# A graph layer's gathers of edge rows: the fourth tile of each group with 127 rows in place of 128

## The reference

```python
h = relu(layernorm(x))
l0, l1 = h0 @ W_l1_0 * a / 8, (h1 @ W_l1_1) * a / sqrt(32)     # the table, 6250 x 160
w = relu(edge_attr_10 @ W_fc1 / sqrt(10)) * sqrt(2) @ W_fc2 / 10   # 192 weights of each edge
y0, y1 = l0[src], l1[src]                                       # the gather, 206250 rows
m0 = w0 * y0 * e0;            m1 = (w1 * y0)[:, :, None] * e1[:, None, :]
m2 = (w2 * e0)[:, :, None] * y1;  m3 = w3 * einsum('eud,ed->eu', y1, e1) / sqrt(3)
s = segment_sum(m, dst)                                         # for each of m0 to m3
out = x + self_interaction(h) + 0.5 * (linear maps of s) * a
```

## Time and profile before

| | before |
|---|---|
| median of three runs | 2132.71 us |
| the profiled execution, its own time | 2139.31 us |
| span of the profiled execution | 2137.5 us |
| PE busy | 2021.8 us (95%) |
| DVE busy | 1684.6 us (79%) |
| POOL busy | 1576.3 us (74%) |
| ACT busy | 343.0 us (16%) |
| mean granted clock of TensorE | 0.928 |

### The profile page before, as it was taken

How to read it: one execution, slowest core, us unless ns; L and a number is a source line. 1 busy time by engine, 2 the same in 40 slices (tenths; PEclk the granted TensorE clock), 3 DMA queues, 4 the chain that set the end, 5 groups by cost and what they waited for, 6 DMA issues and landing times.

```text
span 2137.5 us, 42022 instructions
## 1 busy us (share of the span) xinstructions
PE 2021.8 (95%) x11466; PEld 1603.7 (75%) x11466; DVE 1684.6 (79%) x4634; ACT 343.0 (16%) x636; POOL 1576.3 (74%) x1637
## 2 busy tenths in 40 slices
PE   6899999999999999999999999999999999999998
PEld 5677777787778778777777777777777777777776
DVE  6478878788787888888877888887888878888786
ACT  4311111111111111111111111111111111111111
POOL 6277777777777777777777777777777777777774
PEclk8699999899998998999998989999999989998998
DMA  4223222223222332232232223233232322322233
GB/s 134 72 70 72 72 72 70 71 71 72 71 72 69 71 72 71 70 73 71 71 103 71 71 71 71 72 71 72 71 71 71 73 70 70 73 72 69 71 72 91
DMA packets 159932, 158.29 MB, mean 74 GB/s; under 512 B 86882, under 2 KB 131846, under 8 KB 159914
## 3 DMA queue, kind: packets, MB, share of 16 engines
q0 software_dynamic: 77376, 132.16, 25.0%
q1 hardware_dynamic: 81400, 24.49, 5.2%
q10 hardware_dynamic: 1138, 1.43, 0.2%
HBM read 149.90 MB, written 8.03 MB: 74 GB/s over the span
## 4 chain that ended last, share of the span: by engine, by line
POOL 31%; issue 25%; DMA 18%; DVE 15%; PE 9%; DVEq 1%; POOLq 1%; ACT 0%; SPq 0%; ACTq 0%
POOL y L361 31%; DMA y<-table,idx 17%; DVE hot L654 5%; DVE msg L630 5%; DVE dot L624 4%; PE ps_s L858 2%; PE ps_w L830 2%; PE ps_s L860 2%; PE ps_h L823 1%; DVE dots L620 1%; PE ps_w L792 1%; DVE stats L520 1%; PE ps_h L781 0%; POOLq L369 0%; DVEq L685 0%
## 5 line engine op out<-in xcount | busy, mean ns | idle before, releaser
L361 POOL DMA_INDIRECT y<-table,idx x1612 | 1541.9, 957 | 536.5 <-issue 490.5
L830 PEld LDWEIGHTS ps_w<-w_fc,hr 100*128 100x128 f32 x3224 | 539.3, 197 | 331.8 <-issue 331.8
L830 PE MATMUL ps_w<-w_fc,hr 100*128 100x192 f32 x3224 | 663.0, 351 | 0.0
L858 PE MATMUL ps_s<-hot,msg 128*128 128x128 f32 x3224 | 485.0, 298 | 67.9 <-DVE msg L640 67.3
L858 PEld LDWEIGHTS ps_s<-hot,msg 128*128 128x128 f32 x3224 | 436.6, 206 | 112.3 <-DVE msg L640 109.0
L459 ACT ACTIVATE hr<-ps_h 100x512 f32<-100x512 f32 x403 | 240.7, 597 | 1681.1 <-PE ps_h L823 1681.1
L823 PE MATMUL ps_h<-rad,w_fc 10*100 10x512 f32 x806 | 464.1, 656 | 5.7 <-DMA rad<-in_radial 5.7
L620 DVE TENSOR_TENSOR dots<-y,attr_sb 128x384 f32<-128x384 f32 x403 | 225.1, 559 | 276.7 <-DMA y<-table,idx 276.3
L860 PE MATMUL ps_s<-hot,msg 128*128 128x64 f32 x3224 | 432.0, 280 | 0.0
L860 PEld LDWEIGHTS ps_s<-hot,msg 128*128 128x128 f32 x3224 | 423.3, 205 | 0.0
L682 DVE TENSOR_TENSOR acc<-acc,ps_s 64x32 f32 (+1 forms) x1612 | 325.2, 202 | 71.6 <-PE ps_s L860 31.1
(11 more groups left out here) (79 smaller groups left out, 527.0 us busy)
## 6 DMA issues: line engine op xcount, KB each, us to landing
y<-table,idx POOLq DMA_INDIRECT x1612
rad<-in_radial SPq DMA_DIRECT2D x202, 40.0 KB
xres<-in_x SPq DMA_DIRECT2D x7, 560.0 KB, 4.2
table<-y SPq DMA_DIRECT2D x6, 560.0 KB, 3.2
out<-xres SPq DMA_DIRECT2D x6, 560.0 KB, 4.7
idx<-in_src SPq DMA_DIRECT2D x202, 4.0 KB
attr_sb<-in_attr SPq DMA_DIRECT2D x202, 16.0 KB
dst_i<-in_dst ACTq DMA_DIRECT2D x1, 808.0 KB, 6.3
```

What stands on the lines that cost most here:

```text
L361: nc.gpsimd.indirect_dma_start(out=y[:, j, t, :], out_offset=None, in_=table, in_offset=bass.IndirectOffsetOnAxis(ap=idx[:, j // HALF, col ...
L830: ins = nc.tensor.matmul(ps_w[:, s, t, 0:NW], hr[:, s, t * P:(t + 1) * P], w_fc2[:, :], start=True, stop=True)
L858: nc.tensor.matmul(ps_s[:, s, 0:4 * W], msg[:, s, t, 0:P], hot[:, s, t, 1:V, :], start=(t == 0), stop=(t == T - 1))
```

## The change

The first three tiles of a group keep 128 edges, the fourth has 127 (`ROWS_OF`), so a group holds 511 edges (`EG`). 206250 edges make 404 groups in place of 403, so LEFT is 4 and not 3; TURNS stays 101, and so does the number of SP's loads. The fourth gather of each group goes over partitions 0 to 126 of `idx` and `y`. So that partition 127 of that tile of `y` holds numbers, POOL sets partitions 96 to 127 of it to zero once, after the table's stores have landed and before the first gather. On the host the edges are laid out anew, with attributes of zero in the row that is not used. The compute instructions keep their shapes: they still go over 128 partitions.

```diff
--- before.py
+++ after.py
@@ -29,10 +29,12 @@
 V = 5
 G = 4
 HALF = 2
-TURNS = -(-E // (P * T * G))
+ROWS_OF = [P] * (T - 1) + [P - 1]
+EG = sum(ROWS_OF)
+TURNS = -(-E // (EG * G))
 GROUPS = TURNS * G
 TILES = GROUPS * T
-EDGE_GROUPS = -(-E // (P * T))
+EDGE_GROUPS = -(-E // EG)
 LEFT = EDGE_GROUPS - (TURNS - 1) * G
 PAIRS = TURNS // 2
 assert TURNS == 2 * PAIRS + 1
@@ -150,6 +152,7 @@
         ld_w = sem("ld_w")
         ld_wnode = sem("ld_wnode")
         zeroed = sem("zeroed")
+        y_zeroed = sem("y_zeroed")
         consts = sem("consts")
         dst_step = sem("dst_step")
         base_bc = sem("base_bc")
@@ -349,6 +352,9 @@
             pool.wait_ge(order_step, 3)
             nc.gpsimd.memset(acc[:, :, :], 0.0).then_inc(zeroed, 1)
             pool.wait_ge(table_out, 16 * STORES)
+            pool.wait_ge(zeroed, 1)
+            nc.gpsimd.memset(y[P - 32:P, :, T - 1, :], 0.0).then_inc(y_zeroed, 1)
+            pool.wait_ge(y_zeroed, 1)
 
             def gather_group(i, j, first):
                 if j % HALF == 0:
@@ -359,8 +365,8 @@
                 for t in range(T):
                     col = (j % HALF) * T + t
                     nc.gpsimd.indirect_dma_start(
-                        out=y[:, j, t, :], out_offset=None, in_=table,
-                        in_offset=bass.IndirectOffsetOnAxis(ap=idx[:, j // HALF, col:col + 1], axis=0),
+                        out=y[0:ROWS_OF[t], j, t, :], out_offset=None, in_=table,
+                        in_offset=bass.IndirectOffsetOnAxis(ap=idx[0:ROWS_OF[t], j // HALF, col:col + 1], axis=0),
                     ).then_inc(gathered[j], 16)
 
             def windowed():
@@ -941,21 +947,30 @@
 
     get = {k: np.asarray(v) for k, v in inputs.items()}
 
-    def by_tile(v, fill):
-
-        padded = np.concatenate([v, np.broadcast_to(fill, (EP - E, *v.shape[1:])).astype(v.dtype)])
-        return np.ascontiguousarray(np.moveaxis(padded.reshape(TILES, P, *v.shape[1:]), 0, 1))
+    row = np.arange(P)
+    in_group = np.stack([sum(ROWS_OF[:t]) + np.minimum(row, ROWS_OF[t] - 1) for t in range(T)])
+    used = np.stack([row < ROWS_OF[t] for t in range(T)])
+    edge = np.arange(GROUPS)[:, None, None] * EG + in_group
+    real = used & (edge < E)
+    edge = np.minimum(edge, E - 1)
+
+    def rows_of_edges(v, unused=None):
+        rows = v[edge]
+        if unused is not None:
+            rows[~real] = unused
+        return rows.reshape(TILES, P, *v.shape[1:])
+
+    def by_tile(v, unused=None):
+        return np.ascontiguousarray(np.moveaxis(rows_of_edges(v, unused), 0, 1))
 
     def padded_rows(v):
         return np.concatenate([v, np.zeros((NP - N, v.shape[1]), v.dtype)])
 
-    radial = np.zeros((N_BASIS, EP), np.float32)
-    radial[:, :E] = get["edge_attr_10"].T
     arrays = {
         "x": np.ascontiguousarray(padded_rows(get["x"])[:, ORDER]),
-        "src": by_tile(get["src"], 0),
-        "dst": by_tile(get["dst"], get["dst"][-1]),
-        "radial": radial,
+        "src": by_tile(get["src"]),
+        "dst": by_tile(get["dst"]),
+        "radial": np.ascontiguousarray(rows_of_edges(get["edge_attr_10"], 0).reshape(EP, N_BASIS).T),
         "attr": by_tile(get["edge_attr_4"], 0),
         "avec": np.ascontiguousarray(padded_rows(get["node_vec1"]).reshape(BLOCKS, P).T),
     }
```

## The result

The change takes 2787.85 us (median of four runs, 2785.25 to 2791.9) against 2132.11 us for the kernel before in the same session (2131.26 to 2132.8): ratio 1.3059, with a 95% interval of 1.303 to 1.3088. It is 656 us slower. The forecast was 2139.0 us, and the range ended at 2260 us.

What follows compares the result with a forecast made beforehand. POOL's issue rate was taken to bound the kernel at 5.045 us a group. +5.7 us (group more and later landing) and +0.6 us (memset) made +6.3 us on 2132.71, so 2139.0 us; range 1960 to 2260 us.

Steps and rivals of the forecast that it cites:

- What bounds the kernel: Edge stage: POOL never waits and its issue rate sets the pace, 5.045 us a group; DVE's floor is about 4.31.
- The 0.016 us: Saving on each fourth gather from which a cheaper price on POOL decides, 6.3 / 404.
- POOL's price of the fourth gather: POOL's time for each gather over 127 partitions: 0.957 us as for 128, no gain and no loss, 404 times.
- Dearer on POOL: Rival: uneven division built row by row lengthens each fourth gather; 0.25 us more gives 2240 us, 0.50 gives 2341; chance 0.22.
- the added group: End of the edge stage: one group more costs +4.1 us at DVE's pace, not POOL's +5.0.
- the landing: Rows of the 127-partition gather land 0 to 4.9 us later; with the group more +4.1 to +7.2, taken +5.7 us.
- the memset: POOL's zeroing between the table's stores and the first gather: between 0 and 0.6 us, taken as 0.6.
- an unchanged price: Main case: fourth gather costs POOL the same as before; own range 2134 to 2142 us, chance 0.36.
- cheaper: Rival: POOL builds 127 rows for less than 0.957 us; 0.3 us saved gives 2018 us, at most 1842; chance 0.34.
- The cover: Inside the loop a later landing costs nothing: the index load has 6.8 us of room, 1.9 after the upper bound.

Runs made afterwards that it cites:

- e1: The changed kernel with the fourth gather over all 128 partitions, the 128th row a repeated one: 2138.91 us, ratio 1.0008 to the kernel before.
- e8: The changed kernel with the fourth gather over 120 partitions, seven edges of each group left out: 2170.79 us.
- e2: The changed kernel with the fourth gather over 126 partitions, the rows of the 127th edge left out: 2176.6 us.
- e4: The changed kernel with the fourth gather over 122 partitions, five edges of each group left out: 2477.45 us.
- e5: The changed kernel with the fourth gather, still over 127 partitions, fetching 64 bytes a row in place of 640: 2846.22 us.
- e7: The changed kernel with the fourth gather over 64 partitions, 63 edges of each group left out: 2215.3 us.
- e3: The changed kernel with the fourth gather over 124 partitions, three edges of each group left out: 2360.24 us.
- f1: The kernel before with a small memset on POOL and a wait for it ahead of each group's second gather: 2500.86 us, ratio 1.1702.
- f2: The kernel before with a small memset on POOL and a wait for it ahead of each group's fourth gather: 2401.23 us, ratio 1.1236.

## Why the prediction was wrong

**What bounds the kernel: right.** POOL's issue rate set the pace before and does after; it never waits in either. The 0.016 us at which the price of a gather decides followed from it, and every run bore it out: what the gathers lengthen by is what the kernel lengthens by. The span less the gathers' busy time is 595.6 us before (2137.5 - 1541.9), 596.8 with the change and 590 to 602 in e1 to e8.

**The step that failed: "POOL's price of the fourth gather".** I took 0.957 us from the nearest row, "same opcode, one row of 128 less", and bounded it from above by the dearest gather seen, 1.456 us. It took 2.55 us in the mean, +1.59 us, 404 times, some 644 of the 656 us. Nothing in the trace of before varied the division among the engines, so the row of 128 partitions was near in rows and far in what it costs: 8 steps against 127. The rival "Dearer on POOL" named the mechanism, a build row by row, with 0.22; its price, up to +0.50 us, was three times too small, because I let the longest gather seen stand for an upper bound. Those long gathers are stretched by DVE and say nothing about the build: in the trace of before 48 gathers are over 0.1 us longer than the others, 47 of them begin while DVE is in dots or hot, the longest, at 674.95, 0.04 us after hot, and the 48th is the first of all. The text said that nothing excludes more, and then the range ended at 2260 us all the same.

The forecast did say slower, with 0.59, but that it came out so is luck: 6.3 us were to come from the added group, the landing and the memset, none of which made the loss.

The number of engines was in the rule that I cited, from the Trainium skill, page "DMA: Bandwidth & Descriptors", section "Why a DMA increments its semaphore by 16 and not by 1": one engine for 127 partitions. The trace agrees that a single engine moves the rows (18 full packets and one row for a gather, 4 us of movement more), and the packets of e2 to e4 and e8 show its divisors 14, 4, 2 and 15. I used it for the landing alone, +1.5 us, and did not ask what it does to the engine that builds the descriptors.

**The landing: mechanism right, size near.** The upper bound was 4.9 us later than 2.53; it came 5.5 us later (8.06), of which 1.6 us are the longer build. The movement after the build is 3.9 us longer. The cover held: SP issues the load of indices just behind the landing,

```profile
1312.88 0.35 SPq L276 DMA_DIRECT2D idx<-in_src  x1
```

and POOL reads them from 1320.72 on, after the fourth gather of 1317.87, still 6.1 us after they land by the earlier trace rows (1312.88 + 1.69). It takes no part in the loss: e5 landed 2.2 us earlier and was no faster.

**The added group and the memset: not settled by the times.** Without the landing's share of 1.6 us they were to cost 4.7 us; e1 measures 2.3 us (-1 to +5), so neither that nor zero is excluded. The memset took 0.63 us, as computed.

**The range.** Two steps of the working are loose. At an unchanged price the terms run from +4.1 to +7.8 us, which gives 2136.8 to 2140.5 us, not 2134 to 2142. And an even spread of "cheaper" (0 to 0.74 us saved) and "dearer" (0 to 0.50 us more) over their bounds puts 0.40 of each outside 1960 to 2260 us, not a third and a quarter: 0.14 + 0.09 + 0.04 = 0.27 in place of 0.20. Neither would have reached 2788 us.

**What is not settled.** The 0.04 us that a division over fewer than 16 engines costs in the gather itself and in the one behind it is measured (e2, e8), its cause is not. That POOL's time goes with the rows of the fullest engine is shown; that it does so because POOL writes an order for every engine at each step is my reading of the placeholders, and no run separates it from another cause that grows with these rows.

## What to carry to other kernels

Give an indirect gather a number of partitions that 16 divides, padding it if need be: one repeated row made 2788 us into 2139. What counts is the number of rows that the fullest DMA engine gets. 127, which no number from 2 to 16 divides, is the worst of those tried; 122 with 2 and 124 with 4 cost more than 126 with 14, so fewer rows can cost more. And look at what the new times do to the start of the other gathers: e7, with 16 engines and the cheapest fourth gather of all, lost 82 us by it. When a bound for an unseen form is taken from "the dearest row seen", ask first whether that row is dear for a reason that has anything to do with the form.

## What the runs showed of the hardware that I had not expected

- The queue holds placeholders for the DMA engines that take no part: for 127 rows 20 packets on each of 16 engines, 320 in all, where 128 rows need 48. A step costs about 0.013 us (e3 to e4 0.0127, e4 to the change 0.0133).
- A gather that begins while DVE is in an operation with two operands in SBUF (dots 0.56 us, hot 0.68 us) is stretched, to 1.32 us when it begins 0.06 us after dots (e7) and 1.45 us when 0.05 us after hot (f1). One that has begun before it is not: in the kernel before, the second gather starts at 1026.25 and takes its usual 0.95 us, while the rows land at 1026.28 by the earlier trace rows and dots follows at 1026.31:

```profile
1026.25 0.95 POOL L361 DMA_INDIRECT y<-table,idx  x1 [0.30 <-issue]
1026.31 0.56 DVE L620 TENSOR_TENSOR dots<-y,attr_sb 128x384 f32<-128x384 f32 x1 [0.78 <-DMA y<-table,idx]
```

  The Trainium skill, page "GPSIMD Engine Reference", section "Key points", says that the two engines contend when DVE works with two SBUF inputs; the traces agree (the table behind f2), and add that it is the start of the gather that counts. The kernel before escapes by 0.06 us of timing in this group, and in 333 of its 403 groups the second gather begins within 0.2 us ahead of dots. In e7, whose fourth gather is 0.05 us shorter and lands its rows 0.2 us earlier (2.38 us after its start in place of 2.60, in the median), 311 of 404 begin inside dots, and it lost 82 us.
